# Graph network on one core: the aggregation of a graph as three rounded products in place of one in full fp32

## The reference, cut to what matters

```python
for l in range(attn_w.shape[0]):                    # 3 layers
    si = x @ attn_w[l, :d]
    sj = x @ attn_w[l, d:]
    scores = si[:, :, None] + sj[:, None, :] + attn_b[l]
    scores = jnp.where(scores >= 0, scores, 0.2 * scores)
    scores = jnp.where(mask, scores, -jnp.inf)
    attn = jax.nn.softmax(scores, axis=-1)
    agg = jnp.einsum('bij,bjd->bid', attn, x)
    h = layernorm(x + agg, g1[l], beta1[l])
    ff = jax.nn.gelu(h @ W1[l] + b1[l], approximate=False) @ W2[l] + b2[l]
    x = layernorm(h + ff, g2[l], beta2[l])
```

## Time and profile before

| | before |
|---|---|
| time, median of 3 runs | 1662.7 us (1662.7 to 1662.86) |
| the profiled execution's own time | 1662.55 us |
| its span | 1660.6 us |
| TensorE busy | 1620.2 us (98%) |
| VectorE busy | 1342.2 us (81%) |
| ScalarE busy | 1229.5 us (74%) |
| GpSimd busy | 1333.2 us (80%) |
| mean granted TensorE clock | 0.996 |
| DMA | 127.63 MB, mean 77 GB/s |

### The profile page before, as it was taken

How to read it: one execution, slowest core, us unless ns; L and a number is a source line. 1 busy time by engine, 2 the same in 40 slices (tenths; PEclk the granted TensorE clock), 3 DMA queues, 4 the chain that set the end, 5 groups by cost and what they waited for, 6 DMA issues and landing times.

```text
span 1660.6 us, 40201 instructions
## 1 busy us (share of the span) xinstructions
PE 1620.2 (98%) x12064; PEld 1440.2 (87%) x12064; DVE 1342.2 (81%) x5322; ACT 1229.5 (74%) x2851; POOL 1333.2 (80%) x2376
## 2 busy tenths in 40 slices
PE   9999999987999999999999999999999999999997
PEld 8888888866989989898898989989889898998986
DVE  5899999997777777778877777778888888888865
ACT  5888888885776777777777676777777787787874
POOL 8688888864777877778787787877878999999996
PEclk9999999999999999999999999999999999999999
DMA  6234233212122212212122221211212122222211
...
DMA packets 141721, 127.63 MB, mean 77 GB/s; under 512 B 12240, under 2 KB 132560, under 8 KB 141648
## 3 DMA queue, kind: packets, MB, share of 16 engines
...
...
## 4 chain that ended last, share of the span: by engine, by line
PE 72%; DVE 3%; POOL 1%; issue 0%; ACT 0%; POOLq 0%; DVEq 0%; ACTq 0%
PE ps L45 32%; PE ps L950 30%; PE ps L922 5%; PE ps L936 3%; DVE gnn_junk L1082 2%; PE ps L914 1%; PE ps L929 1%; DVE gnn_e L1115 0%; POOL n L169 0%; DVE gnn_res L1145 0%; DVE xo L1193 0%; DVE res L1125 0%; POOL gnn_inv_last L884 0%; ACT gnn_w_hi L1038 0%; DVE gnn_st L1130 0%
## 5 line engine op out<-in xcount | busy, mean ns | idle before, releaser
L950 PE MATMUL ps<-gnn_w_hi,gnn_g_hi 128*128 128x256 f32 x1536 | 434.0, 283 | 1.5 <-DVE gnn_res L1145 1.5
L950 PE MATMUL ps<-gnn_w_lo,gnn_g_hi 128*128 128x256 f32 x1536 | 428.9, 279 | 0.0
L950 PE MATMUL ps<-gnn_w_hi,gnn_g_lo 128*128 128x256 f32 x1536 | 428.7, 279 | 0.0
L1050 ACT ACTIVATE gnn_g_hi<-ps,b_cols 128x512 fp32r<-128x512 f32 x384 | 264.3, 688 | 199.3 <-PE ps L45 199.3
L1153 DVE TENSOR_TENSOR gnn_g_lo<-ps,gnn_g_hi 128x512 fp32r<-128x512 f32 x384 | 262.9, 685 | 109.8 <-ACT ps L1051 109.8
L45 PE MATMUL ps<-gnn_hT_hi,gnn_w_hi 128*128 128x512 f32 x768 | 337.9, 440 | 0.0
L45 PE MATMUL ps<-gnn_hT_lo,gnn_w_hi 128*128 128x512 f32 x768 | 303.6, 395 | 0.0
L45 PE MATMUL ps<-gnn_hT_hi,gnn_w_lo 128*128 128x512 f32 x768 | 303.5, 395 | 0.0
L950 PEld LDWEIGHTS ps<-gnn_w_hi,gnn_g_hi 128*128 128x128 f32 x1536 | 288.7, 188 | 3.9 <-DVE gnn_res L1145 1.7
L950 PEld LDWEIGHTS ps<-gnn_w_lo,gnn_g_hi 128*128 128x128 f32 x1536 | 288.9, 188 | 2.3
L950 PEld LDWEIGHTS ps<-gnn_w_hi,gnn_g_lo 128*128 128x128 f32 x1536 | 288.7, 188 | 0.0
...
## 6 DMA issues: line engine op xcount, KB each, us to landing
...
```

Source lines behind the costliest of these rows:

```text
L950: mm = e.matmul(FF2[j % 2], g[a][:, m, j * N:(j + 1) * N], W2[b][:, m, :], start=(n == 0), stop=(n == len(terms) - 1))
L1050: e.activation(g[0][:, m, :], FF1[FFB[m]], ACT.Gelu, bias=bias)
```

## The change

`pT` (now two tiles, high and low, of the rounded type fp32r) and `x` (two new tiles `xs`, high and low) are both split, and each aggregation is three matmuls on the rounded parts. ScalarE's `copy_pT` now writes the high part of `pT`, and a new `x_hi` on ScalarE rounds `x` of step `t+2` behind the exponentials. VectorE gets `pT_lo` at the start of a step and `x_lo` behind `residual2` of graph 1. The aggregations of graphs 0 and 1 move from behind block 0 to behind block 1. On VectorE `residual1`, `stats1` and `mean_variance1` stand one block later. `y2` and `norm` use the buffers of the first stage's `y`, and `b2_rows` lies with the first stage's tiles.

```diff
+            pT = [sb("pT_hi", [P, GROUP, N], F32R), sb("pT_lo", [P, GROUP, N], F32R)]
+            xs = [sb("xs_hi", [P, GROUP, XW], F32R), sb("xs_lo", [P, GROUP, XW], F32R)]
...
-                for par in range(2):
-                    e.memset(x[par][:, :, D:XW], 1.0).then_inc(x_ones, 1)
+                for part, value in enumerate((1.0, 0.0)):
+                    e.memset(x[part][:, :, D:XW], value).then_inc(x_ones, 1)
+                    e.wait_ge(x_ones, 2 * part + 1)
+                    e.tensor_copy(xs[part][:, :, D:XW], x[part][:, :, D:XW]).then_inc(x_ones, 1)
...
                 def aggregate(t1, par1, j):
                     if j == 0:
+                        e.wait_ge(x_lo_out, t1 + 1)
                         e.wait_ge(pT_out, t1 + 1)
                     if j >= 2:
                         e.wait_ge(y1_out, GROUP * t1 + j - 1)
-                    e.matmul(AGG[j % 2][:, 0:XW], pT[:, j, :], x[par1][:, j, :], start=True, stop=True).then_inc(agg_made, 1)
+                    for n, (a, b) in enumerate(((0, 0), (0, 1), (1, 0))):
+                        mm = e.matmul(AGG[j % 2][:, 0:XW], pT[a][:, j, :], xs[b][:, j, :], start=(n == 0), stop=(n == 2))
+                    mm.then_inc(agg_made, 1)
...
-                            for j in {0: (0, 1), 3: (2,), 4: (3,)}.get(m, ()):
+                            for j in {1: (0, 1), 3: (2,), 4: (3,)}.get(m, ()):
                                 aggregate(t1, p1, j)
...
-                    e.copy(pT[:].rearrange("p j n -> p (j n)"), TB).then_inc(pT_out, 1)
+                    e.copy(pT[0][:].rearrange("p j n -> p (j n)"), TB).then_inc(pT_hi_out, 1)
+                def x_hi(t2, par2, half2):
+                    e.wait_ge(g_ld[par2], 32 * (half2 + 1))
+                    if not isinstance(t2, int) or t2:
+                        e.wait_ge(agg_made, GROUP * t2)
+                    e.copy(xs[0][:, :, 0:D], x[par2][:, :, 0:D]).then_inc(x_hi_out, 1)
...
                     if more >= 2:
                         exps(t + 2)
+                        x_hi(*ahead(q, par, 2))
...
+                def x_lo(t2, par2):
+                    e.wait_ge(x_hi_out, t2 + 1)
+                    e.tensor_tensor(xs[1][:, :, 0:D], x[par2][:, :, 0:D], xs[0][:, :, 0:D].bitcast(F32),
+                                    ALU.subtract).then_inc(x_lo_out, 1)
+                def pT_lo(t1):
+                    e.wait_ge(pT_hi_out, t1 + 1)
+                    e.tensor_tensor(pT[1][:].rearrange("p j n -> p (j n)"), TB,
+                                    pT[0][:].rearrange("p j n -> p (j n)").bitcast(F32), ALU.subtract).then_inc(pT_out, 1)
...
+                    if more >= 1:
+                        pT_lo(t1)
                     for m in range(FT):
                         gelu_lo(t, m)
-                        if more >= 1 and m == 0:
+                        if more >= 1 and m == 1:
                             e.wait_ge(n1_out, t1)
-                        if more >= 1 and m < GROUP:
-                            residual1(t1, p1, m)
                         if more >= 1 and 1 <= m <= GROUP:
-                            stats1(t1, m - 1)
-                        if more >= 1 and m == GROUP:
+                            residual1(t1, p1, m - 1)
+                        if more >= 1 and 2 <= m <= GROUP + 1:
+                            stats1(t1, m - 2)
+                        if more >= 1 and m == GROUP + 1:
                             mean_variance1(t1)
                         if more >= 2 and m == 5:
                             masked_sums(t2, p2, h2)
...
                     residual2(t, par, 1)
+                    if more >= 2:
+                        x_lo(t2, p2)
```

More of the change, by code:

```diff
@@ L1293, in _ @@
                 attention_shifts(0, 0, first_s[0][0])
+                x_lo(0, 0)
                 split_w1_lo(0, 0)
                 probs_max(0)
+                pT_lo(0)
                 split_w1_lo(0, 1)
```

12 lines of the change are left out of this document (7 added, 5 removed).

## The result

| | before | after |
|---|---|---|
| time, median | 1662.78 us (1662.70 to 1662.91, 4 runs) | 1715.18 us (1714.16 to 1717.49, 4 runs) |
| ratio | | 1.0317, interval 1.0299 to 1.0335 |
| span of the profiled execution | 1660.6 us | 1715.5 us |
| TensorE, VectorE busy | 98%, 81% | 96%, 84% |
| ScalarE, GpSimd busy | 74%, 80% | 74%, 80% |

The account below looks back on a forecast made before the run. TensorE was taken to bound the kernel, with 72% of the chain. Terms 1 to 6 summed as -14.6 + 14.1 + 20.7 + 4 + 18.6 + 4.6 = +47.4, giving 1710 us, range 1676 to 1742 (own case 1690 to 1728).

Parts of the forecast that it names:

- term 2: First aggregation of each step: TensorE waits 0.3 for pT_lo, 47 steps, +14.1 us.
- term 4: Splits of x in layers 0 and 1: nothing in steady steps, 0.6 to 0.8 lost at layer ends, +4 us.
- term 3: ffn2's block 7: the new order makes its low part late, TensorE waits 0.45 in 46 steps, +20.7 us.
- term 6: Ahead of the loop and step 0: the first aggregations wait behind the added splits, +4.6 us.
- Term 1: Aggregation matmuls: three rounded ones at 0.355 replace one fp32 at 0.44, 0.31 saved a step, -14.6 us.
- term 5: Last layer: x_lo has no gap, so hT_lo and pT_lo come later, 12 steps of 1.55, +18.6 us.
- Rival A: VectorE's operations between blocks 4 and 7, and pT_lo, close up so TensorE never waits: 1653 us, chance 10%.
- B: Last layer's longer step gives VectorE time for x_lo, term 5 goes, others at lower ends: 1684 us, chance 22%.
- D: Three rounded matmuls may be no faster than one fp32, each waiting for its weights: 1749 us, chance 5%.
- C: GpSimd's work holds up x_lo on VectorE, which takes 3.5, 2.0 more: 1774 us, chance 8%.

Follow-up runs that it names:

- e8: Changed kernel with the aggregations and statistics back in the old order, x_lo and pT_lo made for step 0 only: 1655.44 us, ratio 0.9957.
- e4: Changed kernel with pT_lo made for step 0 only, later steps reading the old low part of the weights: 1688.94 us, ratio 1.0157.
- e1: Kernel before with the change's order alone, full fp32 and no splits: 1677.14 us, ratio 1.0087.
- e12: Kernel before with its tiles placed as in the changed kernel, same instructions in the same order, no splits: 1667.38 us, ratio 1.0031.
- e7: Changed kernel with masked sums and shifts one block later, pT_lo behind the last residual2, x_lo behind hT_lo in last layer and layer ends: 1694.6 us, ratio 1.0194.
- e10: e7 with the attention sums of graphs 2 and 3 behind the second statistics in all layers: 1668.11 us, ratio 1.0032.

## Why the prediction was right, and where not

The forecast was the case that came true: 1710 for 1715.2, by the mechanisms it named. The steady steps of layers 0 and 1 are 26.51 long on average (26.3 to 26.5 forecast, 25.93 before), those of the last layer (33 to 44) 27.8 (27.9 forecast). The closeness is in part luck: terms 2 and 4 came out 6.5 too small together and term 3 5.7 too large, and term 6 reached its size by a cost that was not in it. Its terms against the ledger:

- **Term 1** (-14.6): right. -14.2 over 46 steps in e8, 0.31 a step. In the changed kernel the blocks save only 8.0, because 3.3 of waiting for `pT_lo` and 1.5 of the clock in step 0 stand inside them; 1.4 more, 0.03 a step, is there without `pT_lo` too (e4) and stays open. The estimate by the Trainium skill (TensorE: Matmul & The Clock Gate, "Back-to-back issue gap"), 4 to 5 us more, did not come: the Trainium skill gives that formula for a matmul by itself, which makes 0.110, and here L927 is 0.119 to 0.120 from L927, nearer the row of 0.117.
- **Term 2**, and the part of `pT_lo` in term 5 (14.1 + 9 = 23.1): mechanism right, 27.6 measured (25.0 before the aggregation and 6.2 behind it, less 3.6 in step 0, which is term 6). The aggregation waits 0.76 to 0.93 in nearly all of the last layer's steps. Steady steps wait 0.20 and 0.44 in turn, and 0.07 more on the next row; why in turn stays open.
- **Term 3** (+20.7): mechanism right, size too large: 15.0. "4.52 after 859.03" was the step: VectorE needs 4.36 (877.84 to 882.20). I had measured the pieces from the start of their first row to the end of their last. In a chain without a wait the next row starts 0.07 to 0.08 before that end, so the 1.44 is 1.37 (to 879.21) and the 0.93 is 0.84 (to 880.06). With that the first row of block 7 is late by 0.39 - 0.16 + 0.06 = 0.29, and 0.27 was measured. The second row adds 0.11, which I had not priced, so the wait is 0.38 in steady steps, and 0.28 in the last layer and at the layer ends. Rival A rests on just this closing up, but there was 0.16 to close, and 0.45 was wanted.
- **Term 4** (+4) was 6.0 at the layer ends: the steps with the w2 split wait 0.55 and 0.69 (0.6 forecast), and that with the w1 split 1.76 in place of 0.8. Nothing in steady steps, as said. Two waits that I had not foreseen stand behind the layer ends: in steps 16 and 32 TensorE waits 1.76 and 0.97 before the transposes of `h`. VectorE's attention sums wait there for a load, by the waits of the changed kernel:

```profile
DVE gnn_junk L1097 <- DMA aw<-in_L_gnn_attn_w: 1.8, 2, 1.2
```

  A wait of this kind is in no answer of before. SyncE issues the loads of step `t+3` when `residual1` is through, which the change puts one block later; e1, with the order alone, has such a wait too (0.8), and TensorE waits 1.16 in its step 16. Before, there are ten small waits before the transposes, 0.16 to 0.48 each and 3.8 in all, in step 0 and around the layer ends. Most of that goes as the two come (3.9 in all after), so the sum hides it.
- **Term 5**, the head of the step in the last layer (12 x 0.8 = 9.6): right, 9.7. `x_lo` took 1.74 there, and the first attention sum 0.95, as said.
- **Term 6** (+4.6): 4.8, but by luck. The loop starts 1.2 later (2.4 forecast) and step 0 waits 2.15 before the aggregation (2.5 forecast, 0.3 of it in term 2); the other 1.5 in step 0 is the granted clock of 0.50, which the prediction did not have.
- **"`y2` and `norm` in other buffers, `b2_rows` elsewhere: nothing, no instruction differs"** was wrong: e12 shows 5.2 us of time and 6.0 in ffn2. It is the largest step that failed in kind, and it makes most of the 7.5 us by which the span was forecast too short; what terms 2 and 4 have too little and term 3 too much nearly cancels.

In the order of the sum: -14.2 + 27.6 + 15.0 + 6.0 + 9.7 + 4.8 + 5.8 = 54.7, where the prediction had 47.4 and the span grew by 54.9. The range of the forecast's own case was added up wrongly: the bounds of terms 3, 5 and 6 give 1695 to 1731, not 1690 to 1728. The measured time lies in both.

Of the rivals, B did not come: the last layer's steps are 27.8 on average. D did not come: e8. C had the right neighbour and the wrong victim. `x_lo` keeps its median of 1.515 (highest 1.805) beside GpSimd:

```profile
L1135 DVE TENSOR_TENSOR gnn_xs_lo<-x,gnn_xs_hi x48: 1215/1515/1805, 384.6 to 1649.9; 128x1024 fp32r<-128x1024 f32 x48
```

so it does not suffer by piece. But GpSimd waits for `x_lo` and passes the delay on, to the later attention sums (e7) and in the last layer to `n` (e10). The Trainium skill (SBUF — State Buffer, "Who interferes with whom") says that a VectorE instruction with two SBUF inputs and a GpSimd one that reads SBUF contend for a shared port that is an exclusive lock. That names both sides, and I had priced only VectorE's. L832's stretch of 0.95 (3.81 less 2.86) agrees with that rule: its second instruction starts at 931.44, while `x_lo` runs to 932.56, and takes 1.72 in place of 0.74.
